# Next batch's first norm, transposes and even q, k projection with its rotation, moved into the stretch between two attention units

## The reference

```python
x = x + attn(layernorm(x))     # 8 heads, each with two score maps of depth 16
x = x + ffn(layernorm(x))      # a recurrent cell over the 16 batches

# attn: q, k = x @ Wq.T, x @ Wk.T, rotated by position tables; v = x @ Wv.T
# probs = softmax(q k^T) for 16 maps; diff = probs[:, :, 0] - lam * probs[:, :, 1]
# out = diff @ v, scaled by its root mean square per head, then @ Wo.T

# ffn, step t = batch t, with xt its 1024 x 256 rows:
ft = sigmoid(xt @ wf.T + c @ uf.T + bf)
it = sigmoid(xt @ wi.T + c @ ui.T + bi)
gt = tanh(xt @ wc.T + c @ uc.T + bc)
c = ft * c + it * gt
# after the last: h = tanh(x @ wo.T + c_final @ uo.T + bo)
```

## Time and profile before

| what | us |
|---|---|
| median of 3 runs | 5066.09 (5051.86 to 5078.93) |
| the profiled execution, its own time | 5038.04 |
| its span in the trace | 5036.2 |
| even attention of one batch (window 1662.36 to 1765.10) | 102.74 |
| odd attention (1773.20 to 1875.28) | 102.08 |
| stretch between the units (1875.28 to 1960.61) | 85.33 |
| TensorE busy, share of the span | 97% |
| VectorE, ScalarE, GpSimd | 78%, 57%, 58% |

### The profile page before, as it was taken

The page is one execution under the profiler, slowest core; times in us unless marked ns, Lnnn a source line. Parts: engine busy times, 40 slices in busy tenths (PEclk is TensorE's granted clock), DMA queues, the critical chain, the costliest instruction groups (busy, mean ns, idle before and its releaser), DMA issues.

```text
span 5036.2 us, 67238 instructions
## 1 busy us (share of the span) xinstructions
PE 4882.4 (97%) x24784; PEld 1744.3 (35%) x24784; DVE 3941.1 (78%) x6295; ACT 2882.7 (57%) x5221; POOL 2937.2 (58%) x2134
## 2 busy tenths in 40 slices
PE   6999999999999999999999999999999999999999
PEld 2224242332423333242332424233242433324237
DVE  6988878888887878878888887888888788887526
ACT  1464646656465665646566464665646566564642
POOL 3583837757384674828568383765738477482740
PEclk7899999999999999999999999999999999999999
DMA  6121231303223130222312123230312313022117
GB/s 147 30 60 53 47 66 45 67 37 65 50 47 72 34 76 37 53 64 47 72 35 58 51 47 66 51 68 31 68 47 48 71 34 76 39 48 55 68 51 291
DMA packets 127723, 311.19 MB, mean 62 GB/s; under 512 B 27297, under 2 KB 30498, under 8 KB 113442
## 3 DMA queue, kind: packets, MB, share of 16 engines
q1 hardware_dynamic: 124178, 289.33, 24.2%
q10 hardware_dynamic: 3216, 17.57, 0.9%
HBM read 172.07 MB, written 99.61 MB: 54 GB/s over the span
## 4 chain that ended last, share of the span: by engine, by line
PE 78%; POOL 11%; ACT 5%; issue 3%; DVE 3%; DMA 0%; ACTq 0%; SPq 0%; DVEq 0%; POOLq 0%
PE s_ps L777 15%; PE o_ps L817 15%; PE st L804 14%; PE st L910 13%; POOL pair_sum L484 11%; PE sum_ps L832 8%; PE st L745 4%; PE st L763 4%; ACT probs L581 3%; PE st L987 2%; DVE neg_max L1107 2%; PE st L888 1%; PE o_ps L732 1%; PE s_ps L987 1%; PE sum_ps L732 0%
## 5 line engine op out<-in xcount | busy, mean ns | idle before, releaser
L484 POOL TENSOR_TENSOR pair_sum<-probs 128x512 f32<-128x512 f32 x2048 | 2829.0, 1416 | 1185.6 <-ACT probs L581 1185.6
L1107 DVE TENSOR_REDUCE neg_max<-s_ps 128x1 f32<-128x512 f32 x4096 | 2582.8, 682 | 705.5 <-PE s_ps L777 703.2
L581 ACT ACTIVATE probs<-st 128x512 f32<-128x512 f32 x4096 | 2161.3, 604 | 960.4 <-PE st L804 797.2
L777 PE MATMUL s_ps<-k_stack,q_stack 96*128 96x512 bf16 x4096 | 1518.6, 388 | 22.5 <-DVE neg_max L1107 21.0
L804 PE MATMUL st<-q_stack,k_stack 99*128 99x512 bf16 x4096 | 1473.3, 384 | 28.7 <-ACT probs L581 7.5
L817 PE MATMUL o_ps<-probs,values 128*32 128x512 f32 x8192 | 1092.4, 605 | 12.3 <-ACT probs L581 8.5
L804 PEld LDWEIGHTS st<-q_stack,k_stack 99*128 99x128 bf16 x4096 | 367.5, 97 | 1357.4 <-ACT probs L581 910.1
L777 PEld LDWEIGHTS s_ps<-k_stack,q_stack 96*128 96x128 bf16 x4096 | 400.3, 98 | 657.5 <-DVE neg_max L1107 315.3
L832 PE MATMUL sum_ps<-pair_sum,ones 128*32 128x512 f32 x4096 | 535.0, 594 | 27.3 <-POOL pair_sum L484 27.3
L910 PE MATMUL st<-pair_sum,weights 128*128 128x512 f32 x768 | 381.9, 594 | 11.8 <-ACT pair_sum L537 11.8
L531 ACT ACTIVATE probs<-st,gate_bias 128x512 f32<-128x512 f32 x192 | 131.6, 686 | 441.8 <-PE st L910 441.8
(11 more groups left out here) (151 smaller groups left out, 3042.2 us busy)
## 6 DMA issues: line engine op xcount, KB each, us to landing
q_stack<-qk_parts SPq DMA_DIRECT2D x384, 128.0 KB, 4.4
k_stack<-qk_parts SPq DMA_DIRECT2D x378, 128.0 KB, 7.0
swapped<-xa SPq DMA_DIRECT2D x128, 256.0 KB, 2.4
qk_parts<-swapped SPq DMA_DIRECT2D x64, 512.0 KB, 2.8
xa<-in_x SPq DMA_DIRECT2D x16, 1024.0 KB, 6.1
qk_parts<-low_part SPq DMA_DIRECT2D x64, 256.0 KB, 3.0
probs<-in_x SPq DMA_DIRECT2D x16, 1024.0 KB, 9.9
x_rows<-probs SPq DMA_DIRECT2D x16, 1024.0 KB, 3.8
```

The costliest lines, as they stand in the source:

```text
L484: pool.tensor_tensor(pair_sum[q % 2][:, h, :], probs[a % 4][:, h, :], probs[(a + 1) % 4][:, h, :], ALU.add)\
L581: act.activation(probs[kk % 4][:, h, :], st[n % BANKS][:, :], ACT.Exp).then_inc(exp_done, 1)
L777: pe.matmul(s_ps[i % BANKS][:, :], q_stack[g][0:SROWS, s, t * P:(t + 1) * P], k_stack[g][0:SROWS, s, h * HALF:(h + 1) * HALF], start=True, ...
L1107: dve.tensor_reduce(neg_max2[:, at, i % 2:i % 2 + 1], s_ps[i % BANKS][:, :], AX.X, ALU.max, negate=True).then_inc(max_done, 1)
```

## The change

For the 14 batches that have a batch b + 2, everything that leads to the even unit's q and k of batch b + 2 is done in the stretch behind batch b's odd attention, and their rotation too.

- VectorE takes the row statistics in steps 26 to 31 of the odd attention (`ROWS_AT`) and the seven small operations right behind it. GpSimd's `next_scales` stands ahead of the two `inv_sqrt_half`.
- ScalarE normalises, and TensorE transposes, before and behind the second half of the output rows; then the q, k projection, ahead of all gates.
- The swap DMAs follow the store of x2 on SP, the store of q's parts follows that of `xt_cols`, and that of k's parts follows `shift_rows`.
- VectorE does nine of the ten rotation operations among the last 15 late maxima (`ROPE_BESIDE`), and the tenth after the first cell sums. The four casts stand ahead of the takes of gates 0 to 3.
- The even attention has no rotation and no casts left. The 8 early scores that stood beside the q, k projection are in its plan, 108 scores in place of 100.
- The transposes of the second norm's first half stand ahead of gate 2, and the turned maxima ahead of gate 6, not 5.
- In the prologue GpSimd rotates unit 2 as well (`rope(2)`).
- Ring places are numbered by `slot` and `taken` in place of `ring_base`, `act_base` and `act_index`.

```diff
-QK0, QK1, WO, GATE, GEE = 0, 4, 16, 20, 32
-VAL = (8, 9, 13, 14)
-RMS = (10, 11, 12, 15)
+FIRST_QK0, FIRST_QK1, FIRST_VAL, NEXT_QK0, PRE = 0, 4, 8, 12, 16
+QK1, WO, QK0, GATE, GEE = 0, 12, 16, 20, 32
+VAL = (4, 5, 9, 10)
+RMS = (6, 7, 8, 11)
...
+def slot(b, i):
+
+    n = PRE + b * PER_ITER + i
+    if b == NB - 1:
+        n -= LAST_RMS[0] + GATE - QK0
+    if b >= NB - 2 and i >= GATE:
+        n -= GATE - QK0
+    return n
+ADDED = {slot(b, WO + j): 4 * b + j + 1 for b in range(NB) for j in range(4)}
+def taken(n):
+
+    return n + 1 - sum(1 for m in ADDED if m <= n)
...
-EARLY = (20, 8)
-BEFORE = EARLY[0]
+BEFORE = 20
-ROPE_AT = ({1: 0, 2: 1, 3: 2, 4: 7, 5: 8, 6: 4, 7: 9, 9: 6, 13: 11, 16: 13},
-           {5: 0, 6: 1, 7: 2, 8: 7, 9: 8, 10: 4, 12: 9, 13: 6, 16: 11, 20: 13})
-CAST_AT = ({4: 3, 7: 5, 11: 10, 14: 12}, {9: 3, 12: 5, 14: 10, 18: 12})
+ROPE_AT = {5: 0, 6: 1, 7: 2, 8: 7, 9: 8, 10: 4, 12: 9, 13: 6, 16: 11, 20: 13}
+CAST_AT = {9: 3, 12: 5, 14: 10, 18: 12}
+ROWS_AT = {26: (0, 1), 28: (2, 3), 29: (4,), 30: (5, 6), 31: (7,)}
+ROPE_BESIDE = ((0, 0), (1, 1), (2, 1), (7, 2), (8, 1), (4, 2), (9, 2), (6, 3), (11, 3))
-WORK = [[(ROPE_WORK if s in at else 0) + (4 if s > 8 and s % 8 == 3 else 0)
-         for s in range(STEPS)] for at in ROPE_AT]
+ROW_WORK = 0.6
+WORK = [[4 if s > 8 and s % 8 == 3 else 0 for s in range(STEPS)] for g in range(G)]
+for s in range(STEPS):
+    WORK[1][s] += ROPE_WORK * (s in ROPE_AT) + ROW_WORK * len(ROWS_AT.get(s, ()))
-PLAN0 = score_plan(sum(EARLY), SCORES, 0)
+PLAN0 = score_plan(BEFORE, SCORES, 0)
...
+                if b < NB - 2:
+                    swap(u + 4, slot(b, QK0))
                 if not last:
-                    sp.wait_ge(xt_out, 4 * (2 * b + 3))
+                    sp.wait_ge(xt_out, 4 * (own(b) + 1))
                     sp.dma_start(xt_scr[b, :, :], flat(xt2)).then_inc(xt_kept, 16)
+                if b < NB - 2:
+                    store_part(u + 4, 0)
+                if not last:
                     shift_rows(u + 2, 0)
+                if b < NB - 2:
+                    store_part(u + 4, 1)
...
+                if following:
+                    for h in range(2):
+                        normalise_next(b, range(4 * h, 4 * h + 4))
+                        take_xt(own(b) - 1, xt, (h,))
+                    take_qk(slot(b, QK0), 2 * b + 4, 0)
+                take_xt(own(b), xt2, (0,))
+                casts = {(0, 0, 0): (3,), (0, 0, 1): (5,), (0, 0, 2): (10,), (0, 1, 0): (12,)}
...
                 pe.wait_ge(at_norm, 4 * b + 4)
-                rows_out(WO, W_O, attn_t, b, ab, js=(2, 3))
+                if following:
+                    transposes(xa, ln1_out, b + 2, own(b) - 1, halves=(0,))
+                rows_out([slot(b, WO + j) for j in (2, 3)], W_O, attn_t, js=(2, 3))
+                if following:
+                    transposes(xa, ln1_out, b + 2, own(b) - 1, halves=(1,))
+                    pe.wait_ge(xt_out, 4 * own(b))
+                    qk(0, slot(b, QK0))
...
                 for i in range(BANKS):
-                    turn(GATE + i, b, ab)
+                    if i == BANKS - 1:
+                        transposes(xn2, ln2_out, b, own(b), halves=(0,))
+                    turn(slot(b, GATE + i))
...
+                    if following is not None and s in ROWS_AT:
+                        dve.wait_ge(x_in, 16 * (following + 1))
+                        norm_rows(xa, ROWS_AT[s])
...
+                if following:
+                    norm_stats(b + 2, -0.5)
...
-                maxima(u + 2, late, LATE[3])
                 normalise_half(b, 1, x2, xn2)
+                for step, n in ROPE_BESIDE:
+                    if following:
+                        rope(u + 4, (step,))
+                    maxima(u + 2, late, n)
                 if not last:
-                    maxima(u + 2, late, LATE[4])
                     join_max(u + 2)
-                    if b < NB - 2:
-                        dve.wait_ge(x_in, 16 * b + 48)
-                        norm_stats(b + 2, xa, -0.5)
                     split_shift(u + 2)
...
                     cell_sum(b, 0, m)
+                if following:
+                    rope(u + 4, (13,))
                 maxima(u + 3, early, 7)
```

More of the change, by code:

```diff
@@ L181, in ring @@
             return st[n % BANKS][:, :]
-        tail_ps = [ring(ring_base(NB - 1, True) + GEE + j) for j in range(3)] + [s_ps[2][:, :]]
+        tail_ps = [ring(slot(NB - 1, GEE + j)) for j in range(3)] + [s_ps[2][:, :]]
         first_in = sem("first_in")
@@ L248, in build, with own @@
         block = ctx.enter_context(nc.Block())
-        def act_base(b, last):
-            return b * ACT_ITER + (PRE - (PRE if last else 0))
+        def own(b):
+            return 2 * b + (3 if b < NB - 2 else 2 if b == NB - 2 else 1)
         def flat(buffer):
@@ L274, in value, with swap @@
                 return v if isinstance(v, int) else sp.lower_val(v)
-            def swap(u, g, ab):
-                first = isinstance(u, int) and u == 0
-                raw_out = [value(ab + (QK1 if g else QK0) + 2 * X + 2) for X in range(2)]
+            def swap(u, first):
                 for X in range(2):
-                    sp.wait_ge(act_out, raw_out[X])
-                    if not first:
+                    sp.wait_ge(act_out, taken(first + 2 * X + 1))
+                    if u > 0:
                         sp.wait_ge(parts_out[X], 32 * u)
@@ L627, in iteration @@
                     if not last and i == 2:
-                        take_v(rb, VAL, (2, 3))
-                own = 2 * b + (1 if last else 2)
-                take_xt(own, xt2, (0,))
+                        take_v([slot(b, VAL[j]) for j in (2, 3)], (2, 3))
                 def normalise_next(b, ts):
@@ L750, in qk, with rows_out @@
                         mm.then_inc(ring_ready, 1)
-            def rows_out(first, w, src, b, ab, js=range(4), beside=(0, 0, iter(()))):
+            def rows_out(slots, w, src, js=range(4), beside=(0, 0, iter(()))):
                 un, un_group, blocks = beside
-                for j in js:
-                    i = first[j] if isinstance(first, tuple) else first + j
-                    turn(i, b, ab)
+                for n, j in zip(slots, js):
+                    turn(n)
                     for t in range(2):
-                        dst = bank(i, b, ab)[:, t * E:(t + 1) * E]
+                        dst = ring(n)[:, t * E:(t + 1) * E]
                         at = (2 * j + t) * P
@@ L856, in iteration @@
             def iteration(b, last):
-                ab = act_base(b, last)
                 u = 2 * b
-                if not last:
-                    if b > 0:
-                        qk(0, b, ab, ((u + 1, 1, i) for i in range(BEFORE, sum(EARLY))),
-                           (1, 1, 0, 0, 1, 1, 2, 2))
-                    pe.wait_ge(act_out, ab + QK0 + 4)
-                else:
-                    for i in range(BEFORE, sum(EARLY)):
-                        score(u + 1, 1, i)
-                    pe.wait_ge(act_out, ab + PRE)
+                following = b < NB - 2
+                pe.wait_ge(act_out, taken(slot(b, LAST_RMS[0] if last else QK1) - 1))
                 attention(u, 0, u + 1, PLAN0)
@@ L967, in _ @@
             turn_max(0)
-            for i in range(sum(EARLY)):
+            for i in range(BEFORE):
                 score(1, 1, i)
@@ L1009, in _, with norm_rows, norm_stats @@
         def _(dve):
-            def norm_stats(n, src, half=0.5):
-                for t in range(TT):
+            def norm_rows(src, ts=range(TT)):
+                for t in ts:
                     dve.bn_stats(stats[:, t, :], src[:, t * E:(t + 1) * E]).then_inc(ln_stat, 1)
+            def norm_stats(n, half=0.5):
                 even, odd = stats[:, :, 0:3], stats[:, :, 3:6]
@@ L1172, in finish_sums, with attention @@
                 combine(u, g, r)
-            def attention(u, g, un, plan, turned=None):
+            def attention(u, g, un, plan, turned=None, following=None):
                 for s in range(STEPS):
@@ L1189, in attention @@
                         maximum(un, i)
-                    if turned is not None and s in ROPE_AT[g]:
-                        rope(turned, [ROPE_AT[g][s]])
+                    if turned is not None and s in ROPE_AT:
+                        rope(turned, [ROPE_AT[s]])
+                    if following is not None and s in ROWS_AT:
+                        dve.wait_ge(x_in, 16 * (following + 1))
+                        norm_rows(xa, ROWS_AT[s])
             def iteration(b, last):
-                rb, ab = ring_base(b, last), act_base(b, last)
                 u = 2 * b
-                for i in range(BEFORE, sum(EARLY)):
-                    maximum(u + 1, i)
-                attention(u, 0, u + 1, PLAN0, None if last else u + 2)
+                following = b < NB - 2
+                attention(u, 0, u + 1, PLAN0)
                 join_max(u + 1)
```

220 lines of the change are left out of this document (101 added, 119 removed).

## The result

The changed kernel took 5128.41 us (median of four, 5127.06 to 5133.8) against 5065.36 for the kernel before on the same chip: ratio 1.0122, interval 1.0099 to 1.0145. The forecast said 5113, range 5048 to 5150, slower. The direction and the range held, but the number flatters the working. The profiled execution after took 5129.55 us (span 5127.8), 91.5 us more than that of before, and the sum had said +47. The 28 us that I added for the median of before did not come back in the kernel after; they were high times of the kernel before in that comparison (5051.86 to 5078.93), and in the four later ones its median was 5040 to 5042. Timed again beside runs of the kernel before that lay at 5041.84, the changed kernel stood at 5131.11, ratio 1.0174 (1.0161 to 1.0188), and that is the figure with which the experiments are compared.

What follows compares the result with a forecast made beforehand. TensorE, busy in 97% of the span, bounds the kernel, so only its waits change. Terms sum to +4.0 us a batch, x 14 = +56, less one-time gains about +47: 5085, plus 28 for the median gives 5113, range 5048 to 5150.

Steps and rivals of the forecast that it cites:

- Even attention -3.8: Even attention without ropes and casts, with 8 more scores: 3.8 us less per batch of the 4.2 lost before.
- Columns +0.9: Between output rows and the q, k projection: TensorE waits 0.9 us per batch for two copies.
- second-norm columns -0.8: Second-norm transposes, now ahead of the third gate's matmuls, which cover their copies: 0.8 us less per batch.
- Nine ropes +2.5: Stretch: nine ropes of 1.2 us among fifteen late maxima hold TensorE's scores, 2.5 us per batch, bounds 0 and 6.7.
- End of the batch +2.7: Start of next even attention: first exponential waits for VectorE's cell sums, now uncovered by the projection; 2.7 us more per batch.
- Clock +2.9: TensorE's granted clock falls to half speed at the end-of-batch gap in nearly every batch: 2.9 us more, 0 to 3.4.
- Odd attention -0.4: Odd attention with row statistics in its last six steps and fewer five-score steps: 0.4 us less per batch, 0 to 0.8.
- the prediction's own sign: Stated test: the prediction is wrong if, among other signs, the odd attention changes by over 1 us.
- Once: One-time gains: prologue and batch 0's even attention -6.9 us, change to batch 15 with batch 14's wait -2.5.
- the kept clock: Rival 1: granted clock stays at 1.00 at the end of the batch, taking off 41 us: 5072; chance 0.20.
- the closed end wait: Rival 2: the end-of-batch wait does not open, so 2.7 and 2.9 fall away: -78, 5035 us; chance 0.13.
- The third, slower ropes: Rival 3: ropes in the stretch at 1.69 us, or the swap 3 us later: +59, 5172 us; chance 0.12.

Runs made afterwards that it cites:

- the gap filled: Changed kernel plus ten unread matmuls before each even attention's fourth key tile, where TensorE waits for the first exponential; 5104.67 us, ratio 1.0128.
- the faster kernel: Changed kernel with stretch rotation on GpSimd, cell-sum wait before step 2, odd plan starting 2 and 1 scores, even plan 3 and 0; 5004.64 us, ratio 0.9923.
- Single edits against one of two falls: Changed kernel with ten filling matmuls, 5104.67 us, or with odd plan starting 2 and 1 scores, 5107.5 us; both edits in one kernel, 5065.53 us.

## Why the prediction was right, and where it was not

Per batch, without the clock, I had -3.8 + 0.9 - 0.8 + 2.5 + 2.7 = +1.5 for the even attention and the stretch. Measured with the gap filled: +1.34 and +0.91, together +2.25. With the clock, +4.4 was said and +4.26 came.

- **Even attention -3.8.** Too large by 0.7, and that is the whole of what the sum without the clock missed. From the first o_ps group to the next projection 98.0 us pass with the gap filled, against 97.1 of own work by the prediction's count; before it was 99.6 against 95.6. So 4.0 lost became 0.9, a gain of 3.1. The waits on pair sums did go, from 27.3 us to 1.9 in the whole kernel.
- **Columns +0.9, second-norm columns -0.8.** Right: 0.74 in the new place, and no wait in the old one.
- **Nine ropes +2.5.** Right: 2.57 with the tenth and the casts, 1.21 to 1.23 a rope, and the first of them 3.0 us behind the take. The Trainium skill ("SBUF — State Buffer", Who interferes with whom) has a VectorE instruction with two SBUF inputs contend with a GpSimd instruction that reads SBUF, and one with at most one, outside the two-port modes, not contend. The trace agrees on both: 1.21 to 1.23 with GpSimd idle and 2.33 beside the pair sums, and GpSimd's own ropes at 2337 to 2359 ns in all batches, though VectorE's maxima, whose one input lies in PSUM, ran beside them.
- **End of the batch +2.7.** Right in chain, order and size: exponential at T+4.19, wait 2.42, and the first o_ps group at T+6.85 (said: 6.7) once the clock is kept.
- **Clock +2.9.** Right that it falls in every batch, 1 us too dear: 1.5 or 2.75, mean 2.0, because in some batches it lasts only about 3.4 us. The Trainium skill ("TensorE: Matmul & The Clock Gate", HAM oscillation) says that where a wait comes back in every tile, the transition of the clock is paid for every time. The trace agrees for the waits of 2.42 us, one in each batch, and in most batches for the 1.62 us at a second place, which I had not seen. In the page's example the waits are 3 to 5 us; here these shorter ones were enough, and the measurement decides.
- **Odd attention -0.4: the step that failed.** It measured +2.7, and by the prediction's own sign, a change of over 1 us, the working was wrong here. I counted the scores of its last six steps and its steps with five, and did not recount the first steps of the new plan. The one score moved into step 1 waits 1.62 us (1.5 lost) and the clock falls behind it in most batches (1.3 in the mean). The rest of the odd attention gave -0.1, inside the range of 0 to -0.8 that I had for it.
- **Once.** The prologue with batch 0's even attention gave 5.3 (said: 6.9). All from batch 14's last stretch on came 1.8 us shorter in the profiled execution and 4.3 in the second one (said: 2.5), but batch 14's odd attention, which I had left out, has the same plan and cost 2.9.

The sum per batch was +4.0 and came out at +7.0; over 14 batches that is 42 of the 44.5 and 42.3 us by which the profiled executions and the second comparison differ from it. That the median still fell near 5113 is owed to the 28 us on top: a wrong addend of 28 hid most of a missing one of 42. That is luck.

Of the rivals, the kept clock was wrong, and the closed end wait became true only by the edits of the faster kernel. The third, slower ropes, was wrong: none in the stretch took over 1.23 us. The faster kernel shows what the change could do: with both plans eased, the cell-sum wait moved and GpSimd's rotation, each stage is at or below the kernel before but the odd attention (+0.4).

## What to carry to other kernels

When a change alters a number that a planner shares out, print the whole plan before and after and read its first steps; a single operation ahead of a slower queue can cost more than the work that was moved. Moving vector work from one full place to another full place on the same engine gained nothing that the times show; moving it to an engine that idled in the same stretch, though at half the pace, kept all of it. Before work that covers a chain of waits is taken away, ask which wait of the chain is needed where it stands, and move that first.

## What the runs showed of the hardware that was not expected

The granted clock fell to 0.52 to 0.53 behind a single wait of 1.62 us in 10 batches of 13 (in the other three the same wait left it at 1.00), and in 9 of 13 behind two waits of 0.43 and 1.04 us with a few matmuls between; one of 1.34 us in the stretch left it at 1.00. It came back after about 3.4 or about 7 us, which cost 1.5 or 2.75 us, and which of the two came changed with the rest of the batch: with the fall in the odd attention gone, the one in the even attention was the long one in every batch. Single edits against one of two falls brought 26 and 24 us, and both together 66.

When the last rope of VectorE (two inputs in SBUF) and a sum of GpSimd started together, within 0.02 us, one of them took its usual time and the other about 1.1 us more: 1.22 and 2.35, or 2.35 and 1.26. Which one lost varied between batches of one execution, and through the queues behind it that decided 0.75 us of that odd attention.
